# Attention scores of a fused block: from 32x32 tiles of one batch element to 64x64 tiles of two, and the weight sums moved to another bank

## The reference, cut to what matters

```
x      : (128 batches, 32 steps, 256)      cond : (128, 256)
h      = GRU over the 32 steps, started from cond
q,k,v  = h @ W + b, each cut into 4 heads of 64
w      = softmax(q k^T / 2)                 # per batch element and head: 32 x 32
x      = x + (w v) @ Wo + bo
y      = 32 Runge-Kutta steps, coupled by tanh(q) @ coupling^T, started from cond
x      = x + quantised FFN of y             # weights rounded to -1, 0, 1 of their mean size
```

## Time and profile before

| | |
|---|---|
| median of 3 runs | 602.54 us (602.47 to 604.92) |
| time of the profiled execution | 602.0 us |
| its span, first to last instruction | 600.1 us |
| granted clock of TensorE, mean share of full speed | 0.997 |
| PE busy | 571.6 us (95%) |
| DVE, ACT, POOL busy | 499.8, 390.9, 250.8 us |

### The profile page before, as it was taken

How to read it: one execution, slowest core, us unless ns; L and a number is a source line. 1 busy time by engine, 2 the same in 40 slices (tenths; PEclk the granted TensorE clock), 3 DMA queues, 4 the chain that set the end, 5 groups by cost and what they waited for, 6 DMA issues and landing times.

```text
span 600.1 us, 17261 instructions
## 1 busy us (share of the span) xinstructions
PE 571.6 (95%) x6460; PEld 519.0 (86%) x6460; DVE 499.8 (83%) x1523; ACT 390.9 (65%) x959; POOL 250.8 (42%) x399
## 2 busy tenths in 40 slices
PE   9999999999999988999978999999999999999997
PEld 8999999999999887888867888888788887888885
DVE  3777777676777767758789999999999999999996
ACT  3545454454544454455557888888888898888785
POOL 0423323233232244320254556556556555555550
PEclk9999999999999999989999999999999999999999
DMA  8500000000000001410000000000000000000001
GB/s 265 182 2 2 1 1 2 1 1 2 2 1 1 19 3 32 127 42 4 2 1 1 11 20 19 11 19 19 10 19 19 11 20 10 19 19 11 19 19 37
DMA packets 13170, 15.08 MB, mean 25 GB/s; under 512 B 1760, under 2 KB 11296, under 8 KB 13088
## 3 DMA queue, kind: packets, MB, share of 16 engines
q1 hardware_dynamic: 13088, 13.98, 7.2%
HBM read 9.78 MB, written 4.19 MB: 23 GB/s over the span
## 4 chain that ended last, share of the span: by engine, by line
PE 78%; ACT 11%; DVE 8%; issue 3%; POOL 0%; DVEq 0%; ACTq 0%; POOLq 0%
PE PS L475 23%; PE PS L322 18%; PE PS L345 13%; ACT q_s L788 5%; PE PS L406 4%; PE PS L453 4%; PE PS L527 4%; PE PS L548 4%; PE PS L511 2%; ACT k_s L769 2%; PE PS L426 2%; PE PS L385 2%; PE PS L328 2%; DVE PS L1081 1%; ACT PS L772 1%
## 5 line engine op out<-in xcount | busy, mean ns | idle before, releaser
L475 PE MATMUL PS<-k_s,h_s 128*128 128x128 f32 x1024 | 160.7, 285 | 4.7 <-DVE PS L1055 2.5
L475 PEld LDWEIGHTS PS<-k_s,h_s 128*128 128x128 f32 x1024 | 131.7, 191 | 21.9 <-DVE PS L1069 9.8
L322 PE MATMUL PS<-part 128*128 128x256 f32 x900 | 115.6, 286 | 0.0
L322 PEld LDWEIGHTS PS<-part 128*128 128x128 f32 x900 | 109.8, 191 | 0.0
L769 ACT ACTIVATE k_s<-h_s 128x128 f32<-128x128 f32 x256 | 69.0, 306 | 50.4 <-DVE h_s L1170 29.0
L345 PE MATMUL PS<-big,wrk 128*128 128x128 f32 x744 | 88.4, 275 | 1.7 <-DVE big L926 1.7
L345 PEld LDWEIGHTS PS<-big,wrk 128*128 128x128 f32 x744 | 85.8, 192 | 2.3 <-DVE big L926 2.3
L1238 POOL COPY h_s<-big 128x256 f32<-128x256 f32 x32 | 21.5, 671 | 129.2 <-DVE big L926 129.2
L475 PE MATMUL PS<-h_s 128*128 128x128 f32 x384 | 74.2, 275 | 0.0
L475 PEld LDWEIGHTS PS<-h_s 128*128 128x128 f32 x384 | 58.3, 192 | 0.0
L664 ACT ACTIVATE big<-big 128x256 f32<-128x256 f32 x32 | 13.3, 417 | 63.2 <-DVE big L908 63.2
(11 more groups left out here) (188 smaller groups left out, 1226.8 us busy)
## 6 DMA issues: line engine op xcount, KB each, us to landing
out<-q_s SPq DMA_DIRECT2D x32, 128.0 KB, 1.7
x_s<-in_xT SPq DMA_DIRECT2D x14, 256.0 KB, 6.0
k_s<-in_wgT SPq DMA_DIRECT2D x4, 208.0 KB, 3.1
k_s<-in_wuT SPq DMA_DIRECT2D x4, 208.0 KB, 2.6
k_s<-in_wih SPq DMA_DIRECT2D x3, 256.0 KB, 4.1
wrk<-in_whh SPq DMA_DIRECT2D x3, 256.0 KB, 4.9
h_s<-in_wdT SPq DMA_DIRECT2D x3, 256.0 KB, 3.8
x_s<-in_xT SPq DMA_DIRECT2D x4, 128.0 KB, 3.7
```

The lines of the kernel that those rows point to most:

```text
L322: r = pe.matmul(p, y, x, start=i == 0, stop=i == len(passes) - 1)
L475: return pe.matmul(PS[:, m, 0:128], w, x, start=False, stop=True, skip_group_check=True)
```

## The change

`scores(i)` makes 32 calls instead of 64: each takes 64 columns of `q_s` (two neighbouring batch elements) as weights and 64 columns of `k_s` as moving data, and writes a 64x64 tile. Only its two diagonal 32x32 squares are scores; the two others mix two batch elements and are not read. The tiles of a block fill all 512 columns of banks 0 and 1. `keep_scores(i)` therefore copies the diagonal squares by four instructions, one for each 32 partitions, of 512 elements each.

Column 256 + w of bank 1 is now in use by the scores, so the sum of weight matrix w goes to column w of bank 2, which the values also use. `weight_sum(w)` now waits until the first values of its block were copied away (`s_V`, 2w + 11), and `values(i, 1)` of blocks 5, 6 and 7 waits for the mean of the same block (`s_wmean`, i - 4). In return `scores(6)` and `scores(7)` no longer wait for a mean, and `feats_of(7)` waits for the last copy of scores instead of the last mean.

```
             def scores(i):
                 if i:
                     pe.wait_ge(s_sc, i)
-                    if i >= 6:
-                        pe.wait_ge(s_wmean, i - 5)
...
                     for kk in range(2):
-                        for j in range(4):
-                            at = (4 * i + g) * 128 + 32 * j
+                        for j in (0, 64):
+                            at = (4 * i + g) * 128 + j
                             for a in (0, 64):
-                                r = pe.matmul(PS[quads[j], a // 64, (2 * g + kk) * 32:(2 * g + kk + 1) * 32],
-                                              q_s[a:a + 64, kk, at:at + 32], k_s[a:a + 64, kk, at:at + 32],
+                                r = pe.matmul(PS[j:j + 64, a // 64, (2 * g + kk) * 64:(2 * g + kk + 1) * 64],
+                                              q_s[a:a + 64, kk, at:at + 64], k_s[a:a + 64, kk, at:at + 64],
                                               start=True, stop=True)
...
+                if hf and i >= 5:
+                    pe.wait_ge(s_wmean, i - 4)
...
                 if i == 7:
-                    pe.wait_ge(s_wmean, 3)
+                    pe.wait_ge(s_sc, 8)
...
             def weight_sum(w):
-                pe.wait_ge(s_sc, w + 6)
+                pe.wait_ge(s_V, 2 * w + 11)
                 pe.wait_ge(s_abs, w + 1)
-                pe.matmul(PS[:, 1, 256 + w:257 + w], ones[:, :], wsum[:, w:w + 1], start=True, stop=True).then_inc(s_wsum, 1)
+                pe.matmul(PS[:, 2, w:w + 1], ones[:, :], wsum[:, w:w + 1], start=True, stop=True).then_inc(s_wsum, 1)
...
-                ac.activation(Sc.rearrange("p (r u) n -> p r (u n)", r=2), PS[:, 0:2, 0:256], ACT.Copy,
-                              scale=0.5).then_inc(s_sc, 1)
+                for j, r in enumerate(quads):
+                    pairs = PS[r, 0:2, :].rearrange("p b (u n) -> p (b u) n", n=64)
+                    o = ac.activation(Sc[r], pairs[:, :, j % 2 * 32:j % 2 * 32 + 32], ACT.Copy, scale=0.5)
+                o.then_inc(s_sc, 1)
...
-                ve.tensor_scalar(wmean[:, w:w + 1], PS[:, 1, 256 + w:257 + w], 1.0 / (NI * 256), TINY, ALU.mult,
+                ve.tensor_scalar(wmean[:, w:w + 1], PS[:, 2, w:w + 1], 1.0 / (NI * 256), TINY, ALU.mult,
                                  ALU.max).then_inc(s_wmean, 1)
```

## The result

The changed kernel takes 609.29 us (median of 4 runs, 607.40 to 613.30), the kernel before 602.66 us on the same chip (602.47 to 604.92). The ratio is 1.0114, with a 95% interval of 1.0064 to 1.0165: slower by 6.6 us. The forecast was 605.2 us and a range up to 608.6.

What follows compares the result with a forecast made beforehand. PE was taken as the bound, losing time to late program packets and a lowered clock. Terms 0 - 1.9 + 1.55 + 1.55 = +1.2 us, plus one fall of 1.5, gave +2.7: 605.2 us by the median, range 601.8 to 608.6.

Steps and rivals of the forecast that it cites:

- Scores 1.0 us, 0.22 gained a block: Score matmuls on PE: 1.0 us a block instead of 1.22, gaining 0.22 us where PE is the bound.
- Four copies 2.1 us, 0.5 from start to start: Score copies on ACT: 0.5 us from start to start, 2.1 for four, +1.5 us ahead of DVE's maximum.
- The moved wait 1.7 us, a block 10.4: Blocks 5 to 7: PE waits 1.7 us for the mean before the second values; a block lasts 10.4 us.
- In block 5 the late program is hidden in it.: Block 5: PE's late program ends at about 6.9 us, before the mean at 7.35, so it adds nothing.
- Blocks 0 to 2, result 0: First blocks: the chain comes 1.3 us later but replaces PE's idle for its program; net 0, possibly 2.8 us lost.
- One fall of the clock, +1.5: Stalls in blocks 5 to 7: one drop to the lower clock behind them, costing 1.5 us; chance 0.38.
- two or three falls: Rival: two or three clock drops behind the stalls of blocks 5 to 7, 606.7 or 608.2 us; chance 0.30.
- Sum without a fall, +1.2: All terms without a clock drop: 0 - 1.9 + 1.55 + 1.55 = +1.2 us; as a rival 603.7 us, chance 0.20.
- The rival of a slow array: 64x64 tiles slower than thought, 1.7 us of scores a block, 608.7 us in all; chance 0.07.
- the short copies: Rival: four 32-partition copies in 0.6 us, new wait 0.2 us, program idles largely gone, 597.8 us; chance 0.05.
- ACT as second bound: Blocks 5 to 7: ACT's busy time plus 1.5 us and about 1 us of waiting stays under 10.4, so no bound.

Runs made afterwards that it cites:

- tiles alone: Changed kernel with weight sums back in the scores' bank and one 128-partition copy (half the squares wrong): 596.85 us, ratio to before 0.9917.
- tiles alone with the one wait added: 64x64 tiles, one copy, sums in the scores' bank, but the weight sum also waits for the first values' copy: 599.47 us, ratio to before 0.9964.
- tiles with the copies: Changed kernel with weight sums back in the scores' bank, so four copies but no moved wait: 603.42 us, ratio to before 1.0020.
- The run without a low clock: Changed kernel with seven dummy 512-column matmuls before each wait for the mean: profiled execution 606.60 us, median 608.32 us.
- the kernel of the late blocks: 64x64 tiles and four copies in blocks 3 to 7 only, weight sums under the scores: 601.18 us, ratio to before 0.9976.
- split copy: 64x64 tiles, sums under the scores; ACT copies left halves scaled by a column, DVE adds right halves, all blocks: 598.00 us, ratio to before 0.9938.
- one run: Changed kernel with one 128-partition copy in place of four, the moved wait kept (half the squares wrong): 602.30 us, ratio to before 1.0009.

## Why the prediction was wrong, step by step

The mechanisms that it named are nearly all there. The step that failed is the term for the clock: one fall at +1.5 us, where the profile after has four low stretches that cost 8.7 us. The waiting, +1.2 in the prediction, came to 2.7, for block 5 was not hidden and blocks 6 and 7 were 0.5 us longer each than forecast.

- *Scores 1.0 us, 0.22 gained a block.* Measured 1.09, and 0.17 gained in block 3. Right. (The 1.22, 1.62 and 1.41 that it takes from the earlier trace rows are 1.28, 1.51 and 1.50 there; their sum is the same within 0.1.)
- *Four copies 2.1 us, 0.5 from start to start.* Measured 2.40 and 0.60, the upper bound. This mis-sized term carries on: the mean ends at 7.82 instead of 7.35, of which 0.3 is the copies.
- *The moved wait 1.7 us, a block 10.4.* The idle is 1.72 and 1.71, as forecast. Without a low clock blocks 6 and 7 lose 1.98 and 2.00 us each (277.19 - 266.37 = 10.82, against 8.84 in the earlier trace rows; then 19.73 to the warm-up matmuls against 17.73), not 1.55. The idle came out right although the mean is late, since PE was late too, above all at the weight sum, where it waited for ACT.
- *"In block 5 the late program is hidden in it."* Wrong. The packet's end fell where forecast, at record 126, but the idle grew to 1.85 us and PE went on at 8.00 us (262.78 - 254.78), after the mean, instead of at 6.9. The step took the time of a packet's arrival as given; the change put later events ahead of it, and tiles alone with the one wait added show that this lengthens the idle by 0.9 us, tiles with the copies by 1.6. scores(6) starts at 267.44 in place of the forecast 263.75. Of these 3.7 us, 1.4 is the clock (values and projection 4.43 us instead of 3.03) and 1.4 is inherited from block 3 (254.78 against 253.35); the values start 0.9 later in their block than forecast (8.23 instead of 7.35), behind this idle.
- *Blocks 0 to 2, result 0.* Without a low clock that was nearly right (235.75, 0.40 early), but as a sum of two terms that were left out: tiles alone win 2.1 us there and the copies cost 1.8. The copies also put a wait of 1.66 us for ACT in block 1, and in the profiled run the clock was low behind it, which cost 1.9 us (237.64). The prediction warned of the late block 1 as a loss of waiting and did not think of the clock there.
- *One fall of the clock, +1.5.* This is the step that decided. The trace has four low stretches, from 219.9, 264.3, 274.5 and 288.2 us, 27 us in all, and they cost 8.7 us by the estimate above, at least 6.6. The prediction priced a fall by the one seen in block 5, where 4.56 us stood for 3.03; behind the mean 5.39 us stand for 3.03 (275.41 to 280.80), +2.4. It weighed falls at three places and chose one; the rival "two or three falls" at 606.7 and 608.2 was the right one by its kind and still too small, by the price and by block 1. In the median of the four runs the clock is less: 6.6 us less the 2.7 of waiting leaves some 4 us, an estimate, still well over 1.5.
- *Sum without a fall, +1.2.* The profile after less its low stretches gives +2.7: -0.40 up to block 3, -0.50 in blocks 3 and 4 (forecast -0.44), -0.59 in block 5 where -1.45 was forecast, and +2.07 and +2.08 in blocks 6 and 7 where 1.55 was. The run without a low clock has +4.7; without the 1.7 us of dummies in block 5 and the 0.9 in block 4 it is +2.1.

The rival of a slow array is refuted by 1.09 us, the short copies by 2.40 (its sum also takes off 0.44 us twice, for the 1.9 holds them already). ACT as second bound was dismissed too quickly: with four copies PE waited for ACT by 0.17 us in blocks 5 to 7, and by 0.41 and 0.51 in the kernel of the late blocks.

The Trainium skill (ScalarE: Activation LUTs, "What ACT_TABLE_LOAD costs") puts an activation without pointer operands at 186 ns and 0.833 ns an element. For 512 that is 613 ns, an estimate; the trace agrees with 0.60 us. Each pointer operand adds about 93 ns by the page, and the copy that is scaled by a column took 0.69 instead of 0.60 us. But its overlap of about 93 ns between activations in a row would make four copies 2.2 us, an estimate; the rows show 2.40 and no overlap.

Why did the forecast miss the gain of tiles alone? It gave blocks 0 to 2 nothing and the others 0.22 each, some 1 us in all, where the experiment found 5.5: 2.1 up to block 3, and 2.3 in block 5 (9.52 us instead of 11.85), where most of the idle and the low clock went. In blocks 0 to 2 three of the four idles for the program went with half the score records. In block 5 the packet still ends at the same record; why its idle shrank from 1.22 to 0.55 us there is not shown.

## What to carry to other kernels

Where an engine outruns its own program, count instructions and not only array time, and look at the waits just ahead of a packet's end, for a later event there can make the next packet later. Do not count one idle as cover for another wait before a run has shown it: here, with 32x32 tiles and four copies, 1.3 of 3.1 us of waits were hidden in blocks 0 to 2. Price a stall on TensorE with what the clock does after it, by the slowest group of matmuls that can stand behind it, and expect the price to vary from run to run. When a faster operation needs companions (more copies, another bank), time each companion alone: here the tile was worth 5.5 us, and two companions ate 12.0; a split of the copy between two engines kept 3.3. Time them beside the change and not only on the kernel before, where these two cost 2.9.

## What the runs showed of the hardware

- A copy of 512 float32 elements takes 0.60 us on ACT with 32 partitions as with 128, and four in a row take 2.40.
- 64 records of float32 64x64x64 tiles take 1.09 us, 17 ns each, though each alone lasts 218 ns; 128 records of 32 columns take 1.22.
- One wait more, just ahead of a packet's end, lengthened the program's idle from 0.55 to 1.43 us; four copies, the last of which is waited for there, lengthened it to 2.19.
- Slow matmuls followed idles of 1.08 us (split copy, block 5) to 2.19 us in many places and not others: 1.66 us in block 1 brought a low clock in the profile after and none in the run of 606.60 us, 1.08 us brought one in block 6 and 1.07 none in block 7 of one run. What decides between them stays open; four runs of the changed kernel, at mean clocks of 0.994 to 0.978, lie 5.9 us apart.
- 64 more records at the start of the program, of one column each with full weights, cost 12 us: they took 10.4 us themselves, 163 ns each, with a low clock from 9.4 to 19.6 us. Why so long was not tried.
